# Gated delta attention: the triangular inverse in 32-wide diagonal blocks, four at a time in tiles of the array, against 64-wide blocks

## What is computed

```
mixed = silu(causal_conv4(h @ w_qkv));  q, k, v = split(mixed)
z = h @ w_z;  beta = sigmoid(h @ w_b);  g = -exp(A_log) * softplus(h @ w_a + dt_bias)
q = l2norm(q) / sqrt(128);  k = l2norm(k)
def step(S, (q, k, v, g, beta)):          # over the tokens
    S = S * exp(g)
    S = S + outer(k, (v - k @ S) * beta)
    return S, q @ S
y = rmsnorm(o * silu(z)) * norm_w;  out = y @ w_out
```

## Time and profile before

| | |
|---|---|
| Runs of the kernel before | median 6047.01 us of 3 (6041.28 to 6048.38) |
| The profiled execution | span 6046.2 us; no other time of its own is given |
| PE, PEld busy | 5221.5 us (86%), 3893.8 us (64%) |
| DVE, ACT, POOL busy | 3480.2 us (58%), 3055.8 us (51%), 1178.3 us (19%) |
| DMA | mean 17 GB/s |
| Granted TensorE clock in the four stages read below | 1.00 |

### The profile page before, as it was taken

The page is one execution under the profiler, slowest core; times in us unless marked ns, Lnnn a source line. Parts: engine busy times, 40 slices in busy tenths (PEclk is TensorE's granted clock), DMA queues, the critical chain, the costliest instruction groups (busy, mean ns, idle before and its releaser), DMA issues. The chain is left out here.

```text
span 6046.2 us, 91895 instructions
## 1 busy us (share of the span) xinstructions
PE 5221.5 (86%) x32318; PEld 3893.8 (64%) x32318; DVE 3480.2 (58%) x6531; ACT 3055.8 (51%) x8923; POOL 1178.3 (19%) x1352
## 2 busy tenths in 40 slices
PE   5799999999989999989999699899998597399969
PEld 4477777877877778877887555555555354255545
DVE  3466666676666667666766566555552554543331
ACT  2466666666656666666666344344441244325421
POOL 0222222322222222222232100011110321002210
PEclk7799999999999999999999799899999798688879
DMA  2000000000000000000000100100000100000000
GB/s 85 19 19 17 13 19 19 18 17 17 19 19 13 17 19 19 17 14 19 22 19 13 46 1 1 65 1 0 0 0 20 27 1 13 21 1 1 1 21 14
DMA packets 51094, 103.57 MB, mean 17 GB/s; under 512 B 12848, under 2 KB 20176, under 8 KB 49520
## 3 DMA queue, kind: packets, MB, share of 16 engines
q1 hardware_dynamic: 50672, 98.07, 5.4%
HBM read 90.43 MB, written 5.52 MB: 16 GB/s over the span
## 5 line engine op out<-in xcount | busy, mean ns | idle before, releaser
L896 ACT ACTIVATE dh_pb<-bank 64x128 f32<-64x128 f32 x3072 | 831.4, 271 | 272.5 <-PE bank L670 239.3
L684 PE MATMUL bank<-dh_cw,dh_pb 128*128 128x128 f32 x5120 | 701.5, 281 | 113.0 <-ACT dh_pb L896 111.4
L684 PEld LDWEIGHTS bank<-dh_cw,dh_pb 128*128 128x128 f32 x5120 | 635.5, 193 | 191.1 <-ACT dh_pb L896 164.4
L1034 DVE SCALAR_TENSOR_TENSOR dh_kq<-bank,dh_conv_kq,dh_kq 128x511 f32<-128x511 f32 (+2 forms) x408 | 305.4, 749 | 184.8 <-ACT dh_kq L853 173.6
L902 ACT ACTIVATE dh_cw<-bank 128x256 f32<-128x256 f32 x640 | 244.9, 385 | 255.1 <-PE bank L684 247.9
L621 PE MATMUL bank<-hT,dh_w_kq 128*128 128x512 f32 x544 | 276.7, 633 | 83.2 <-DVE dh_kq L1034 75.3
L1034 DVE SCALAR_TENSOR_TENSOR dh_v<-bank,dh_conv_v,dh_v 128x511 f32<-128x511 f32 (+2 forms) x384 | 284.2, 747 | 91.3 <-ACT dh_v L853 82.2
L1797 PE MATMUL bank<-moe_h_split,moe_w 128*128 128x512 bf16 x1200 | 277.1, 381 | 14.6 <-PEq L89 14.6
L633 PE MATMUL bank<-dh_w_vz,hT 128*128 128x256 f32 x1024 | 245.5, 383 | 22.0 <-ACT dh_zs L864 22.0
L1128 DVE TENSOR_TENSOR dh_zz<-dh_zz,bank 128x512 f32<-128x512 f32 x130 | 89.2, 686 | 283.0 <-PE bank L597 281.1
L621 PE MATMUL bank<-hT,dh_w_vz 128*128 128x512 f32 x512 | 242.5, 596 | 8.6 <-DVE dh_v L1034 8.6
(11 more groups left out here) (416 smaller groups left out, 12170.8 us busy)
## 6 DMA issues: line engine op xcount, KB each, us to landing
dh_rates<-delta_rates SPq DMA_DIRECT2D x130, 256.0 KB, 3.6
dh_w_vz<-in_L_wvz SPq DMA_DIRECT2D x17, 512.0 KB, 3.3
mod_w<-in_L_wmod SPq DMA_DIRECT2D x4, 1536.0 KB, 7.0
dh_w_kq<-in_L_wkq SPq DMA_DIRECT2D x18, 256.0 KB, 2.6
dh_wo<-in_L_wo SPq DMA_DIRECT2D x16, 256.0 KB, 4.2
moe_w<-in_L_w13T SPq DMA_DIRECT2D x1, 3200.0 KB, 15.7
later_gates<-mod_gate SPq DMA_DIRECT2D x3, 1024.0 KB, 4.0
gate<-later_gates SPq DMA_DIRECT2D x6, 512.0 KB, 3.4
```

The source lines that it names most:

```text
L684: last = pe.matmul(square(j)[:, b, :, :], pb[j][:, b, :], src[:, :, b, :], start=True, stop=True)
L896: last = act.activation(out[half, :, o, half], src[halves[o], :, half], ACT.Copy)
L1034: dve.scalar_tensor_tensor(y, pj_bank(n)[:, 0:S - i], taps(n)[:, TAPS - 1 - i:TAPS - i], y, ALU.mult, ALU.add).then_inc(s["v_cs" if i < TA ...
```

## The change

1. The diagonal blocks are 32 wide, and there are four. They lie on the four groups of 32 partitions. `level` (after) does for each batch and each group one product with a 32 x 32 weight: 16 products per head and level, five levels, of 32 columns in the first and last and 64 in the three between. The weight is the turned power, and the turn is a 32 x 32-block transpose on DVE (`turn_power`, `start_power`, `turn_inverse`). PE's transposes and ACT's layout into `pb` are gone.
2. Two products join 32-wide blocks to 64-wide ones: `join_left`, an ACT copy (`left_copy`), `join_right`, then `right_copy`. ACT writes the inverse's diagonal blocks by `place`, four copies a head.
3. The masked product kkm x decay is made once, for the whole matrix, by POOL (`product`, 128 x 512, in place of `off_diagonal`), and ACT takes the diagonal blocks out of it (`compact`, four copies a head). `w_prod` and `x_prod` read halves: 64 rows and 64 weight columns, 128 streamed columns as before.
4. `qk_mask` on DVE becomes a plain copy on ACT (`qk_copy`).
5. The four orders are rewritten; the slices of projection work stand in tables (FILL, SCALAR_FILL, VECTOR_FILL) at points 0 to 7 of a stage. `decay` now comes behind the fill at point 5, `rms` behind `product`.

```diff
-    def turn_power(pe, t, i, j):
-    def square_power(pe, t, i, j):
-    def off_diagonal(pool, t, j):
-    def qk_mask(dve, t):
+    def level(pe, t, m, j):
...
+        part = slice(0, 1) if m == 0 else slice(0, 2) if m < LEVELS - 1 else slice(1, 2)
         for b in range(NB):
+            for g in QUADS:
+                last = pe.matmul(square(j)[quad[g], b, part, :], pw[j][quad[g], par, b, :], cw[j][quad[g], par, part, b, :],
+                                 start=True, stop=True)
+    def join_left(pe, t, j):
...
+        for b in range(NB):
+            for g in (0, 2):
+                last = pe.matmul(square(j)[quad[g + 1], b, 0, :], dm[j][quad[g], par, b, quad[g + 1]], pw[j][quad[g], par, b, :],
+                                 start=True, stop=True)
+    def product(pool, t, j):
+        h = hs[j]
+        pool.wait_ge(h["v_et"], order(t) + 1)
+        pool.wait_ge(s["v_kk"], order(t) + 1)
+        after(pool, h["t_w"], t + 1)
+        pool.tensor_tensor(dm[j][:, (t + 1) % 2, :, :], kkm[:, :, :], et[j][:, :, :], ALU.mult).then_inc(h["p_dm"], 1)
...
+        pu(pe, t, 0)
+        if old: qs(pe, t, 1)
+        pu(pe, t, 1)
+        tensor_fill(pe, t, 4)
+        if a:
+            for j in HEADS: ku(pe, t, j)
+        for j in HEADS: join_left(pe, t, j)
+        tensor_fill(pe, t, 5)
+        qk_prod(pe, t)
+        for j in HEADS: join_right(pe, t, j)
+        tensor_fill(pe, t, 6)
+        for j in HEADS: y_turn(pe, t, j)
+        tensor_fill(pe, t, 7)
+        for j in HEADS: w_out(pe, t, j)
...
+        scalar_fill(act, t, 4)
+        for j in HEADS: place(act, t, j)
+        for j in HEADS: left_copy(act, t, j)
+        mean_sq(act, t, 0)
+        scalar_fill(act, t, 5)
+        mean_sq(act, t, 1)
+        qk_copy(act, t)
+        for j in HEADS: right_copy(act, t, j)
+        for j in HEADS: compact(act, t, j)
+        scalar_fill(act, t, 6)
+        for j in HEADS: y_copy(act, t, j)
+        scalar_fill(act, t, 7)
...
+        vector_fill(dve, t, 5)
+        for j in HEADS: decay(dve, t, j)
+        vector_fill(dve, t, 6)
         for j in HEADS: normed(dve, t, j)
+        for j in HEADS: start_power(dve, t, j)
         collect(dve, t)
...
-        for j in HEADS: off_diagonal(pool, t, j)
-        if inner: faded(pool, t, 0)
-        scores(pool, t, 0)
-        if inner: faded(pool, t, 1)
-        scores(pool, t, 1)
+        for j in HEADS:
+            if inner: faded(pool, t, j)
+            scores(pool, t, j)
+        for j in HEADS: product(pool, t, j)
         rms(pool, t)
```

More of the change, by code:

```diff
@@ L657, in qk_prod @@
     def qk_prod(pe, t):
-        pe.wait_ge(s["v_kk"], order(t) + 1)
+        if t >= 0 and rec_chunk(t):
+            pe.wait_ge(hs[1]["v_qs"], carried(t))
+        else:
+            pe.wait_ge(s["v_kk"], order(t) + 1)
         par, c = next_par(t), next_chunk(t)
         each(pe, B_AUX, lambda b: key(par, c, b), lambda b: query(par, c, b)).then_inc(s["t_qk"], 1)
-    def turn_power(pe, t, i, j):
-        h = hs[j]
-        if i:
-            pe.wait_ge(h["a_c"], 5 * t + i)
-        else:
[L667 to L673, removed]
@@ L714, in w_prod @@
         pe.wait_ge(h["a_zs"], t + 1)
-        after(pe, h["p_nt"], t)
-        each(pe, B_REC[j], lambda b: ntoff[j][:, b, :], lambda b: zz[j][:, b, :]).then_inc(h["t_w"], 1)
+        for b in range(NB):
+            last = pe.matmul(bank[B_REC[j]][high, b * P:(b + 1) * P], dm[j][low, (t + 1) % 2, b, high], zz[j][low, b, :],
+                             start=True, stop=True)
+        last.then_inc(h["t_w"], 1)
     def x_prod(pe, t, j):
@@ L720, in x_prod, with qs @@
         pe.wait_ge(h["a_w"], t + 1)
-        each(pe, B_REC[j], lambda b: ttb[j][:, b, :], lambda b: ww[j][:, b, :]).then_inc(h["t_x"], 1)
-    def qs(pe, t, j):
+        for b in range(NB):
+            last = pe.matmul(bank[B_REC[j]][high, b * P:(b + 1) * P], ttb[j][high, b, high], ww[j][high, b, :],
+                             start=True, stop=True)
+        last.then_inc(h["t_x"], 1)
+    def qs(pe, t, j, more=True):
         par, c = rec_par(t), rec_chunk(t)
@@ new lines, in delta_pipeline, with scalar_fill @@
+    SCALAR_FILL = {
[7 rows of a table added]
+    }
+    def scalar_fill(act, t, at):
+        q, a = t // NC, t % NC
+        for kind, n in SCALAR_FILL[a].get(at, ()):
+            if kind == "p": tap(act, q, n)
+            if kind == "s": silu(act, q, n)
+            if kind == "z": silu_z(act, q, n)
+            if kind == "t": squares(act, q, n)
+    def scalar_stage(act, t):
+        for j in HEADS: power_c(act, t, 1, j)
+        v_scaled(act, t, 0)
+        scalar_fill(act, t, 0)
+        v_scaled(act, t, 1)
+        for j in HEADS: power_c(act, t, 2, j)
+        for j in HEADS: z_copy(act, t, j)
+        scalar_fill(act, t, 1)
+        for j in HEADS: power_c(act, t, 3, j)
+        for j in HEADS: w_copy(act, t, j)
+        scalar_fill(act, t, 2)
+        scalar_fill(act, t, 3)
+        scalar_fill(act, t, 4)
[10 more added lines that the diff above has]
+        scalar_fill(act, t, 7)
@@ L1380, in _ @@
                 squares(act, -1, n)
+            qk_copy(act, -1)
+            for j in HEADS: compact(act, -1, j)
         @block.vector
@@ L1406, in _ @@
             query_scale(pool, -1)
+            for j in HEADS: product(pool, -1, j)
     ph.clear()
```

470 lines of the change are left out of this document (172 added, 298 removed), and 17 rows, old and new, of tables (FILL, SCALAR_FILL, VECTOR_FILL).

## The result

The changed kernel takes 6568.72 us (median of 4; 6044.15 for the kernel before beside it): 1.0867 times as long, interval 1.0851 to 1.0884, or 525 us more. The forecast was 6490 with 6100 to 6780. One of the four executions took 9229.12 us at a lower clock (0.72 in place of 0.86); it stands in the median, not in the interval, and the other three lie between 6561.23 and 6569.02.

A forecast was written before the change was run, and what follows sets the result against it. PE was taken to set the pace before, at 86% busy; after the change, engines would stand in line. 6046 + 192 (chain) + 173 (clock) + 83 (issue) = 6494, stated as 6490 us, range 6100 to 6780.

The forecast's parts named there:

- the signs named: If right: stages 52 to 60 us, PE under 75% busy, `rms` and scan waiting, clock under 0.95, two-head levels about 0.9 us.
- PE's work: Inverse on PE, per stage: 13.3 us before, 4.4 plus 2.4 after, so PE's work falls by 6.5 us.
- changes of tiles: PE switching between tiles and whole array: 16 a stage at an estimated 0.15 us, 2.4 us.
- The chain, +192: Engines waiting in line within stages: the four kinds total 205.7 us against 193.7 before, +12.0, sixteen times.
- the first parts: PE-paced stage start, cut at the second `pu`: 30.0, 21.5, 27.0 and 22.0 us for kinds 0 to 3.
- the tails: Rest of each stage through `w_out`, engines in line: 25.5, 28.1, 28.8 and 22.8 us for kinds 0 to 3.
- The clock, +173: After PE's idle stretches before `y_turn`, the clock halves, costing 2.7 us once a stage, 64 times.
- The issue of small products, +83: First parts on PE: 0.06 us a pair would add 10.4 us in four stages; half taken, 5.2, sixteen times.
- The tail hides: Rival: tail work ends before PE's items, so PE keeps the pace; 5630 at best, halfway 5830 us; chance 0.17.
- Chain only: Rival: pauses are broken up and issue is no limit, so only the chain's +192 counts; 6240 us; chance 0.2.
- issue binds: Rival: PE needs 0.06 us for each pair throughout and each tile change drains it; 6730 us; chance 0.2.

The follow-up runs named there:

- e2: The changed kernel with only POOL's `rms` moved ahead of the two `product` calls: 6411.41 us.
- e7: The changed kernel, every instruction kept, with stage-end orders on ACT, POOL, DVE and PE rewritten and POOL's products waiting for `normed`: 5837.57 us.
- e1: The changed kernel with eight extra unread 128 x 128 x 512 products on PE ahead of `y_turn` in every stage: 6524.43 us.
- e3: The changed kernel with every product of the five levels issued twice: 6675.91 us (two executions).
- e6: The changed kernel with `rms`, `y_copy`, `normed` moved forward, plus ACT's `mean_sq` ahead of point 4's items and `place`: 6350.70 us; 6347.44 without the `mean_sq` move.

## Why the prediction was right, and where it was not

**What bounds the kernel.** As put: PE set the pace before, and in the changed kernel the hand-written chain does. The row of `y_turn` (6.7 to 656.1 us) is the clearest sign of it, and e2 and e7 show it by orders alone. Of the signs named, the clock and the waits came as said; the stages took 50.7 to 63.4 us and not 52 to 60. (ACT was busy for 28.6 to 33.4 us in the earlier trace rows, not from 26.9; nothing hangs on it.)

**PE's work.** Forecast 6.8 us for levels, joins and changes of tiles (4.4 + 2.4), measured 3 x 1.02 + 2 x 0.69 + 2 x 0.62 = 5.7 from start to start, against 13.3 before: 7.6 us less. But the items beside the tiles grew. Four full-width products ahead of a level took 0.98 to 1.00 us (1615.30 to 1616.29) in place of 0.89, and a projection between two tiled items 1.91 (1619.20 to 1621.11) in place of 1.72. In kind 0, with the clock at 1.00 in both, PE was busy for 45.49 us before and for 40.14 in e7: 5.4 us less, where 6.5 was forecast. Over the launch PE's busy time fell from 5221.5 to 4901.3 us in e7, 5.0 us a stage with more low clock in it. The gain is real and somewhat smaller than said. It was all lost in the changed kernel; e7, which has it, is 205 us under the kernel before.

**The chain, +192.** Forecast 55.5, 49.6, 55.8 and 44.8 us; measured 58.1, 53.2, 63.4 and 50.7 with the clock in them. Cut at the second `pu`, the first parts were 30.7, 22.3, 31.7 and 24.3 us against 30.0, 21.5, 27.0 and 22.0, and the tails 27.4, 30.9, 31.6 and 26.4 against 25.5, 28.1, 28.8 and 22.8. Where clock and chain are told apart by rows (next point), the four tails are right to 1.3 us in 105, and the first parts 6.8 short. The waits are not what was short: PE was idle for 3.7, 1.0, 5.4 and 1.6 us in them, 11.7 in all, and 14.4 had been put down. PE's work was: 27.1, 21.3, 24.6 (less the clock's 1.7) and 22.7 us against 24.5, 19.3, 22.0 and 20.3, some 9.5 in all. The forecast's first parts count the five levels at their bare 3.5 us (and the list adds up to 24.7, not 24.5); the 2.4 us a stage that the forecast itself had put down for changes of tiles never came into them. Between 2.0 and 2.6 us are missing in each kind, about that amount. `product` was mis-sized too: 1.67 us in the changed kernel, not 1.28. So this term is about 334 and not 192.

**The clock, +173.** In kind 0 turns and `w_out` took 7.41 us where the earlier trace rows give 4.35, 3.1 more; read the same way kind 1 gives 1.4, kind 2 3.7, kind 3 3.3 on the path: 11.5 in four stages, 16 x 11.5 = 184. The size was right, and partly by luck: some 1.7 us of kind 2 come in its first part, behind a pause of 1.91 us of which the forecast had no word, and kind 1 gives half of what was put down. Of the experiments e1 bears this out in kind 1 alone; in the sum of the kinds it gave 44 us back, for the reasons told there.

**The issue of small products, +83.** This step failed. The pace of 0.06 us was read behind a loop boundary, where the queue is empty; in the levels a record takes 0.016 us (64 in 1.02), and e3 shows 0.009 to 0.014 for each more. The term is nothing. The Trainium skill, "TensorE: Matmul & The Clock Gate", section "Wait — 56ns, not 53.3ns?", has 25 ns between starts as the least, and 62 ns where hardware decode is off. Neither is seen with tiles side by side: at 25 ns the 384 records would take 9.6 us, an estimate from the page, and 5.7 were taken. The warning of the Trainium skill's "TensorEngine Tiling (Array Packing)", section "Instruction Overhead", is not borne out as a loss either: halving the columns from 64 to 32 took a level of both heads from 1.02 to 0.69 us, a third off where half of the columns went, but it is a gain.

**The sum.** 192 + 173 + 83 = 448 was forecast, 334 + 184 + 0 = 518 is read off, and 525 measured. Two errors of 140 and 80 us in opposite directions: the time came out within 79 us of 6490, and two of its three terms were off by more than that. That the issue term stood where the changes of tiles were missing is luck.

**The rivals.** "The tail hides" (0.17) was false for the kernel as changed and names what e7 then did by moving the orders: its 5830 is e7's 5838, which is chance in the figure but not in the mechanism. "Chain only" fell with the clock at 0.83 to 0.90 and `w_out` at 5.61 us; "issue binds" with e3.

**What stays open.** How much of e7's gain is the clock and how much the chain: by the rows the clock can be at most the 184 us of 731 that it cost the changed kernel, but no run holds the clock still. And what the kernel before would take with its own order tuned further. PE is busy for 92% of its stages, so that order alone could give it no more than the other 8%, 4% of the launch or some 247 us. That bound, about 5795, is below e7's 5838, so it is not shown that the tiles win over a 64-wide kernel in its best order.

## What to carry to other kernels

When work is taken off the engine that sets the pace, read what hid beneath it: here PE's levels and transposes lay over the output path, and with most of that work gone and the orders changed each item of that path showed. Put the items that lead to the end of the chain first on every in-order engine: one line on POOL gave 157 us (e2), one on ACT nothing, because DVE's order held the chain (e6), and all of them together 731 (e7). Look at the clock before a difference of a microsecond or two in a stage is put down to an order. And judge an arithmetic and its order apart: the same instructions took 6569 and 5838 us.
